# A gated recurrence on one core: the kept part of the state goes to TensorE as one fp32 operand, with idle passes and side work placed anew

## What is computed

```
x = x + ffn0(cond0(x))                       # token-wise, products over all tokens
def step(H, xs):                             # 128 steps, H is 16 x 128
    xz, xr, xh = xs                          # x times Wxz, Wxr, Wxh, with biases
    Z = sigmoid(xz + H @ Whz.T + bhz)
    R = sigmoid(xr + H @ Whr.T + bhr)
    H_tilda = tanh(xh + (R * H) @ Whh.T + bhh)
    H_new = Z * H + (1.0 - Z) * H_tilda
    Y = H_new @ Whq.T + bhq
    return H_new, Y
x = x + expert[argmax(Y @ router.T + b)](Y)  # relu(relu(Y w1 + b1) w2 + b2)
```

## Time and profile before

| | |
|---|---|
| median of three runs | 259.83 us (259.51 to 261.93) |
| the profiled execution | 263.02 us, its span 261.2 us |
| TensorE busy | 250.5 us of the span (96%), weight loads 204.6 (78%) |
| VectorE, ScalarE busy | 218.3 us (84%), 162.7 us (62%) |
| chain that ended last | TensorE 83%, VectorE 10%, ScalarE 3% of the span |
| granted TensorE clock | full from 9.7 to 20.0 us, half to 57.5 us, then full |
| first step's product with `parts`, step (1, 0)'s, step (7, 15)'s | 15.29, 54.68, 251.47 us |

### The profile page before, as it was taken

The page is one execution under the profiler, slowest core; times in us unless marked ns, Lnnn a source line. Parts: engine busy times, 40 slices in busy tenths (PEclk is TensorE's granted clock), DMA queues, the critical chain, the costliest instruction groups (busy, mean ns, idle before and its releaser), DMA issues.

```text
span 261.2 us, 10662 instructions
## 1 busy us (share of the span) xinstructions
PE 250.5 (96%) x3854; PEld 204.6 (78%) x3854; DVE 218.3 (84%) x1528; ACT 162.7 (62%) x826; POOL 15.2 (6%) x29
## 2 busy tenths in 40 slices
PE   6999899999999999999999999999999999999996
PEld 6978788788877788788877777777877777777775
DVE  5776566789998989988998999898988988788983
ACT  3455455557665866677666766587657766556652
POOL 4872000000000000000000000000000000000000
PEclk9995555559999999999999999999999999999999
DMA  7900000000000000000000000000000000000000
GB/s 245 360 15 6 0 3 1 3 0 4 4 3 4 23 1 3 4 24 3 4 4 20 4 3 4 4 23 4 3 1 23 4 4 3 21 5 0 5 23 23
DMA packets 3380, 5.76 MB, mean 22 GB/s; under 512 B 568, under 2 KB 2128, under 8 KB 3328
## 3 DMA queue, kind: packets, MB, share of 16 engines
q1 hardware_dynamic: 2848, 4.24, 4.8%
q10 hardware_dynamic: 432, 0.74, 0.8%
q0 software_dynamic: 48, 0.10, 0.1%
HBM read 4.03 MB, written 1.05 MB: 19 GB/s over the span
## 4 chain that ended last, share of the span: by engine, by line
PE 83%; DVE 10%; ACT 3%; issue 2%; DMA 2%; DVEq 0%
PE ZH L1087 9%; PE R L1087 8%; PE F L1010 6%; PE O L960 6%; PE ZH L1086 5%; PE O L957 3%; DVE parts L866 3%; PE O L916 3%; PE L L1097 2%; PE R L1132 2%; PE L L982 2%; PE O L953 2%; PE O L917 2%; PE O L918 2%; PE R L1086 2%
## 5 line engine op out<-in xcount | busy, mean ns | idle before, releaser
L454 ACT ACTIVATE r_early<-O 128x16 f32<-128x16 f32 x127 | 23.5, 185 | 35.0 <-PE O L960 32.0
L1087 PE MATMUL R<-m_p,gru_hi 128*128 128x16 f16 x254 | 44.2, 175 | 0.0
L487 ACT ACTIVATE ZH<-ZH 128x16 f32<-128x16 f32 x128 | 21.8, 170 | 29.9 <-PE ZH L1087 28.1
L1087 PE MATMUL ZH<-m_p,gru_hi 128*128 128x16 f16 x254 | 36.7, 170 | 0.0
L866 DVE TENSOR_TENSOR_SCAN parts<-factors,terms 128x48 f16<-128x48 f32 x128 | 33.0, 258 | 4.1 <-ACT factors L458 0.5
L837 DVE TENSOR_TENSOR terms<-r_early,factors 128x16 f16<-128x16 f32 x128 | 24.0, 188 | 12.7 <-ACT r_early L454 8.0
L609 DVE SCALAR_TENSOR_TENSOR hid_lo<-F,hid_hi 128x128 f16<-128x128 f32 x112 | 31.9, 285 | 0.2 <-issue 0.2
L458 ACT ACTIVATE factors<-R 128x16 f32<-128x16 f32 x128 | 24.7, 193 | 11.5 <-PE R L1087 0.2
L880 DVE TENSOR_TENSOR m_p<-keep,ZH 128x16 f16<-128x16 f32 x128 | 21.8, 170 | 11.4 <-ACT ZH L487 7.1
L482 ACT ACTIVATE keep<-z_sb 128x16 f32<-128x16 f32 x128 | 28.3, 221 | 2.1
L1086 PEld LDWEIGHTS ZH<-terms,gru_lo 128*128 128x128 f16 x128 | 12.7, 100 | 18.4 <-ACT z_sb L460 15.5
(11 more groups left out here) (270 smaller groups left out, 1057.3 us busy)
## 6 DMA issues: line engine op xcount, KB each, us to landing
w_sb<-w SPq DMA_DIRECT2D x2, 512.0 KB, 8.1
outT<-res SPq DMA_DIRECT2D x7, 128.0 KB, 1.9
xs_sb<-xsT SPq DMA_DIRECT2D x1, 640.0 KB, 9.7
first_sb<-first ACTq DMA_DIRECT2D x1, 279.0 KB, 4.0
ffn_sb<-ffn SPq DMA_DIRECT2D x1, 256.0 KB, 3.8
ffn_sb<-ffn ACTq DMA_DIRECT2D x1, 256.0 KB, 4.8
second_sb<-second SPq DMA_DIRECT2D x1, 256.0 KB, 4.5
xs_sb<-xsT SPq DMA_DIRECT2D x1, 256.0 KB, 6.7
```

What stands on the lines that cost most here:

```text
L454: nc.scalar.activation(r_early[:, p, :], early_r[:, at], ACT.Sigmoid).then_inc(early_made, 1)
L1087: return mm(out, gru_hi[:, WHR + gate, :], part, start=False, stop=low, skip_group_check=True)
```

## The change

- **zh whole.** VectorE makes zh in fp32 alone; its two fp16 parts and their tile fall away. TensorE multiplies it with the fp32 weights in one call each into the early copy, R and Z (`whole`): three fp32 matmuls of 16 columns in place of seven fp16 ones. The product into Z stands behind the first three of m, as the ones that it replaces did.
- **Chunk 0's idle passes.** `stream` passes are added ahead of the terms' product (`spare_first`), between the two candidate products and behind the last one; some numbers of `spare_passes` change.
- **Chunk 0's input.** From step 4 on the early copy's input is made from fp16 parts of x1, which ScalarE and VectorE make in two halves at steps 2 and 6 to 7 (`x1_first_high`, `x1_first_low`), with three matmuls in place of one fp32 one. Weight casts move by some steps for it.
- **Places of y and routing.** y's high part is taken behind the tanh, its low part's second half at step 2, the first places of the routing (`first_places`) both at step 5 ahead of the scan, the second `best_places` at step 4, x1 is evacuated in two halves at steps 6 and 7, and the low parts of the feed-forward layer move by half a step. Waits of TensorE on the O bank follow these (`out_bank_read`).

```diff
-                    nc.vector.tensor_tensor(zh_p[:, q, 0, :], z_sb[:, p, :], h_old, ALU.mult).then_inc(zh_hi, 1)
                     nc.vector.tensor_tensor(zh[:, q, :], z_sb[:, p, :], h_old, ALU.mult).then_inc(zh_full, 1)
                     wide_any(k, t, 0)
-                    dve.wait_ge(zh_full, step + 1)
-                    nc.vector.tensor_tensor(zh_p[:, q, 1, :], zh[:, q, :], zh_p[:, q, 0, :],
-                                            ALU.subtract).then_inc(zh_lo, 1)
...
+            def whole(out, gate, part):
+                mm(out, gru_sb[:, WHR + gate, :], part, start=False, stop=False, skip_group_check=True)
...
             def out_bank_read(k, t):
-                return t == {0: 4, K - 1: 0}.get(k, 6) or t == (12 if k == 0 else 0)
+                if k == 0 and t == 4:
+                    pe.wait_ge(x1_rest_made, 1)
+                if k > 1 and t == 0:
+                    pe.wait_ge(res_made, 2 * k - 3)
+                if k < K - 1 and t == (12 if k == 0 else 6):
+                    pe.wait_ge(x1_made, 2 * k + 2)
...
-                        if out_bank_read(k, t - 1):
-                            pe.wait_ge(zh_lo, step)
+                        out_bank_read(k, t - 1)
                         early_input(k, t)
-                        pe.wait_ge(zh_hi, step)
-                        early_product(t, zh_p[:, q, 0, :])
-                        product(r_out, 0, zh_p[:, q, 0, :])
-                        pe.wait_ge(zh_lo, step)
-                        product(r_out, 0, zh_p[:, q, 1, :], low=True)
+                        pe.wait_ge(zh_full, step)
+                        whole(early_r[:, at], 0, zh[:, q, :])
+                        whole(r_out, 0, zh[:, q, :])
                         pe.wait_ge(m_hi, step)
                         early_product(t, m_p[:, q, 0, :]).then_inc(early_mm, 1)
                         product(r_out, 0, m_p[:, q, 0, :])
                         pe.wait_ge(m_full, step)
-                        product(z_out, 1, zh_p[:, q, 0, :])
-                        product(z_out, 1, zh_p[:, q, 1, :], low=True)
+                        whole(z_out, 1, zh[:, q, :])
                         product(z_out, 1, m_p[:, q, 0, :])
...
-                if k == 0:
+                if k == 0 and t < 4:
                     mm(out, gru_sb[:, WXR, :], x1[:, at], start=False, stop=False, skip_group_check=True)
                 else:
+                    if k == 0 and t in (4, 8):
+                        pe.wait_ge(gru_lo_made, 2)
+                        pe.wait_ge(x1_first_lo, 1 + t // 8)
...
+            def spare_first(passes):
+                stream(L_bank[:, N:2 * N], passes)
             def first_before(t, step):
+                if t > 1:
+                    spare_first({2: 1, 3: 1, 6: 2, 7: 1, 12: 2, 13: 4}.get(t, 0))
...
             def first_between(t):
+                if t in (4, 10, 11, 12, 13):
+                    spare_first(1)
...
-                spare_passes(0, {7: 1, 8: 0, 9: 1, 12: 3, 13: 3}.get(t, 0))
+                spare_passes(0, (1, 1, 1, 1, 1, 1, 0, 1, 1, 1, 1, 1, 3, 3, 0, 0)[t])
...
+            def first_places(q):
+                dve.wait_ge(key_made, 2 * q + 2)
+                if q == 0:
+                    dve.wait_ge(zeros_set, 2)
+                for i in range(2):
+                    above(blocks(pen[:, i, :]), key[:, i:i + 1, :], best[:, i:i + 1]).then_inc(pen_made, 1)
...
+                        if t == 2:
+                            y_low(k - 1, 1)
                         if t == 4:
-                            first_place(k - 1, 0)
-                        if 7 <= t < 15:
+                            best_places(k - 1, 1)
+                        if t == 5:
+                            first_places(k - 1)
+                        if t == 7:
+                            x1_evacuate(k + 1, 1)
+                        if 8 <= t < 15:
                             expert_low(k - 1, t - 7, 0)
```

More of the change, by code:

```diff
@@ L380, in x1_high, with x1_first_high @@
             def x1_high(n):
-                act.wait_ge(x1_made, n + 1)
+                act.wait_ge(x1_made, 2 * n + 1)
                 nc.scalar.copy(x1_hi[:, n % 2, :], x1[:, cols(n)]).then_inc(x1_hi_made, 1)
+            def x1_first_high(half):
+                if half == 1:
+                    act.wait_ge(x1_rest_made, 1)
+                at = slice(half * 128, half * 128 + 128)
+                nc.scalar.copy(x1_hi[:, 0, at], x1[:, at]).then_inc(x1_first_hi, 1)
             def error_function(n):
@@ L471, in _ @@
                         w1_high(3)
-                    if feed and t == (13 if k == 0 else 7):
+                    if feed and t == (13 if k == 0 else 8):
                         x1_high(k + 1)
@@ L492, in _ @@
                         first_relu(1, 2 * t + 1)
-                    if k == 0 and t in (2, 3, 6):
-                        w1_high((2, 3, 6).index(t))
+                    if k == 0 and t == 2:
+                        x1_first_high(0)
+                    if k == 0 and t in (3, 6):
+                        w1_high((3, 6).index(t) * 2)
+                    if k == 0 and t == 15:
+                        w2_high(3)
                     if k == 0 and t == 4:
@@ L500, in _ @@
                         expander(t - 11)
+                    if experts and t == 0:
+                        y_high(k - 1)
                     if experts and t == (4 if last else 5):
@@ L535, in x1_first, with x1_first_low @@
                                                op1=ALU.add).then_inc(x1_rest_made if half else x1_made, 1)
+            def x1_first_low(half):
+                dve.wait_ge(x1_first_hi, half + 1)
+                at = of(half)
+                nc.vector.tensor_tensor(x1_lo[:, 0, at], x1[:, at], x1_hi[:, 0, at],
+                                        ALU.subtract).then_inc(x1_first_lo, 1)
             def low_rank_masked(n, half):
@@ L756, in first_wide @@
                     ffn_low(1, t - 8, half)
+                if t == 2 and half == 1:
+                    x1_first_low(0)
                 if t == 12 and half == 0:
                     dve.wait_ge(xs_next_in, 16)
-                    x1_evacuate(1)
+                    x1_evacuate(1, 0)
+                if t == 12 and half == 1:
+                    twice_gelu(2, 1)
                 if t == 14:
@@ L769, in wide @@
                     finish(k - 2, 0)
-                if t == 1:
-                    y_low(k - 1, half)
-                if 2 <= t < 2 + NF:
+                if t == 1 and half == 0:
+                    y_low(k - 1, 0)
+                if t == 1 and half == 1:
+                    ffn_low(k + 1, 0, 0)
+                if t == 2:
+                    ffn_low(k + 1, half, 1 - half)
+                if t == 3 and half == 0:
+                    best_places(k - 1, 0)
+                if t == 3 and half == 1:
+                    ffn_low(k + 1, 1, 1)
+                if t in (4, 5):
                     ffn_low(k + 1, t - 2, half)
-                if t == 3:
-                    best_places(k - 1, half)
-                if t == 4 and half == 0:
-                    first_place(k - 1, 1)
                 if t == 6 and half == 0:
@@ L780, in wide @@
                         dve.wait_ge(xs_in, 16)
-                    x1_evacuate(k + 1)
-                if 7 <= t < 15 and half == 0:
+                    x1_evacuate(k + 1, 0)
+                if k == 1 and t == 6 and half == 1:
+                    w2_low(7)
+                if t == 7:
+                    expert_low(k - 1, 0, half)
+                if 8 <= t < 15 and half == 0:
                     expert_low(k - 1, t - 7, 1)
-                if t in (7, 8) and half == 1:
-                    x1_low(k + 1, t - 7)
-                if t in (9, 10) and half == 1 and k < K - 3:
-                    low_rank_masked(k + 3, t - 9)
+                if t in (8, 9) and half == 1:
+                    x1_low(k + 1, t - 8)
+                if t in (10, 11) and half == 1 and k < K - 3:
+                    low_rank_masked(k + 3, t - 10)
                 if t in (12, 13) and half == 1 and k < K - 2:
@@ L801, in wide_last @@
                     best_places(K - 2, 1)
-                if t == 3 and half == 1:
-                    first_place(K - 2, 0)
                 if t - 1 in LAST_HIDDEN_AT and half == 0:
@@ L847, in _ @@
                         finish(k - 2, 1)
-                    if k == 0 and t in (12, 13):
-                        twice_gelu(2, t - 12)
                     if k == 0 and t in (14, 15):
@@ L853, in _ @@
                         first_early(t)
-                    if k == 1 and t in (0, 2, 6):
-                        w2_low((0, 2, 6).index(t) + 5)
+                    if k == 1 and t in (0, 1, 6):
+                        w2_low((0, 1, 6).index(t) + 4)
                     if last:
@@ L884, in _ @@
                                             ALU.subtract).then_inc(m_lo, 1)
+                    dve.wait_ge(zh_full, step + 1)
```

(2 more changed lines are left out.)

41 lines of the change are left out of this document (23 added, 18 removed).

## The result

The changed kernel takes 449.3 us (median of four runs, 445.53 to 450.19); the kernel before, on the same chip, takes 260.88 us (259.51 to 261.98). The ratio is 1.720 (95% interval 1.705 to 1.735). The forecast was 290 us with a range of 278 to 318, so slower was right and the size was not: the time lies 131 us beyond the range, at the end that the rival "The clock falls" had given as "up to 450 in all".

The account below looks back on a forecast made before the run. Bound by one chain through VectorE, TensorE and ScalarE, steps of 1.71 us. Profiled 263.0 us plus 33.2 for the 111 steps, minus 2.9 for chunk 0, is 293.3; less 3.2 without profile, 290 us, range 278 to 318.

Parts of the forecast that it names:

- The clock falls: Rival: TensorE drops to half clock; 309 us if in chunk 0, up to 450 if it stays low; chance 20%.
- What bounds the kernel: A single chain through VectorE, TensorE and ScalarE sets an ordinary step's 1.71 us; TensorE has only two small holes.
- the price of a call: Each fp32 matmul of 16 columns on TensorE costs 0.22 us at full clock, two passes of 0.11.
- Loads hidden: Rival: the fp32 passes' weight loads run under earlier matmuls on TensorE, giving 254 to 257 us; chance 6%.
- The step of 2.03: Three fp32 calls push R's last product 0.325 us later, so a step of 1.71 us becomes 2.03.
- The holes' account: TensorE's two holes in a step, 0.08 and some 0.09 us, take up 0.17 of the 0.49 us extra work.
- VectorE's two parts: Removing two VectorE instructions is worth nothing in ordinary steps, 0.1 to 0.2 us only in few steps.
- Moved side work: Both first places ahead of one scan cost 0.2 us in each of six chunks, 1.2 us; other moves nothing.
- Chunk 0: With the clock held at 2.4 GHz, its 16 steps take 36.5 us, a gain of 2.9.

Follow-up runs that it names:

- e1: The changed kernel with eight more idle passes on TensorE at step (0, 5), ahead of its wait; 412.92, 437.57, 414.59 and 345.89 us.
- e8: e5 with more idle passes in chunk 0, zh still in three fp32 calls; 292.73 us, ratio 1.116.
- e9: The changed kernel with seven fp16 products of zh in chunk 0, three fp32 calls from chunk 1 on, and e5's later passes; 286.18 us, ratio 1.091.
- e4: e1 with fp16 products of zh into the early copy and R, leaving only Z's fp32 call; 256.35 us, ratio 0.976.
- e2: The changed kernel with zh's seven fp16 products and VectorE's two parts put back, all else as changed; 250.95 us, ratio 0.954.
- e7: e2 plus four idle fp16 passes of 256 columns in each step where the fp32 calls stood; 280.62 us, ratio 1.069.
- e3: The kernel before with zh whole in three fp32 calls and waits on the O bank as changed, nothing else; 450.77 us, ratio 1.717.
- e6: e1 with two fp32 calls of zh, into the early copy and R, and fp16 products into Z; 396.42 us (345.11 to 397.56).
- e5: The changed kernel with more idle passes in chunk 0, at the later chunks' starts and ends, and in chunk 7; 412.77 us (344.43 to 460.33).

## Why the prediction was right or wrong

**What bounds the kernel; the price of a call.** Right. 0.45 and 0.23 us in the changed kernel at full clock, no hidden loads (the rival "Loads hidden" is out), and the chain behind R's last product unchanged (0.75 for 0.77).

**The step of 2.03.** Right in size: 2.01 in e1's chunk 1, in e8 and e9. The 111 steps take 228.35 us in e8, of which its passes at the chunks' ends are about 0.3 in each chunk (32.89 against 32.58 in e1's chunk 1); the forecast was 230.0. The holes' account was too simple, as e4 showed, but for three calls, two of them ahead of m, it comes out the same.

**VectorE's two parts.** Nothing gained, as said: with m's high part 0.32 us early in e8, VectorE isn't waited for.

**Moved side work.** I charged 1.2 us. e2 shows that together with all else but zh it brings 3.3 us in the 111 steps, of which 0.6 lie where before was still at half clock. Wrong in sign, small.

**Chunk 0.** This is the step that failed: "I take the clock as held: chunks 1 to 7 stay at 2.4 GHz throughout with side work of the same size in a step as chunk 0 now gets." The 111 steps were priced at full clock alone in the same way. Chunk 0 took 50.41 us for the 36.5 of the sum, the 111 steps 367.12 for its 230.0, at 1.2 GHz from 27.2 us on. Side work of the same size was beside the point. With as long a list in chunk 0, but passes in place of the fp32 calls, e7 does keep the clock there and takes 34.4 us, near the 36.5 forecast. The steps of chunks 1 to 7 that kept the clock had seven fp16 products of zh, and the change takes just these away. e3 shows the fp32 calls alone keep the clock from coming back; e7 shows that as long a list with fp16 passes holds it; e4 and e6 show that it turns between one call and two in a step. What the rows offered, and I passed over: before's one long stretch at half clock, 20.0 to 57.5 us, lies in the one chunk in which each step has an fp32 call of 16 columns, the early input. That is a hint and no more, since e4 has such a call in each step and keeps the clock. And I counted as evidence against the rival that the clock never fell in 193.8 us of later chunks, in none of which zh was fp32.

**The rival's number.** Its price was right; what would make the clock fall it didn't say. At half clock a call is 0.43 and the step 3.36 us, for the 3.4 given; a chunk costs 53.63 us against 32.58, 21 more, for the 22 given. That its "up to 450" comes so close to 449.3 is luck: 309 plus seven chunks at 22 is 463, while chunk 0 took 50.41 us for the 55 given and the seven chunks lost about 140 for the 154. What was wrong above all is its 20%, of which I gave half to a fall in chunk 0 alone or a late one, and so a range that ended at 318. Of the 170.3 us that the 111 steps lost, about 30 are the price at full clock (e8's 228.35 less some 2 for its own passes, against 196.79) and about 140 the clock's (367.12 against 226).

**The wait at step (0, 5).** The profile of after points at it, and the timeline of the fall begins there. e7 and e2's trace have the same wait at a held clock; e9 lost the clock right behind it, with fp16 products, and had it back 6.8 us later; e1 and e3 lost it ahead of the wait. It can be the moment of the fall. It is not what keeps the clock down for 409 us.

**Open.** Why e5 gets the clock back at the end of chunk 5 and e8 in chunk 0, with lists that differ by a few passes, and why one program (e1, e5, e6, e9) is at half clock for a different time from run to run, isn't settled. e5, e6 and e7 ran on another chip than the other experiments; the kernel before takes the same time on both (262.49 us there, 262.33 and 262.53 here). Which property of these fp32 calls costs the clock (the loads, the few columns, the two passes) wasn't tried apart.

## What to carry to other kernels

A step that runs at full clock tells nothing of the clock behind a change that replaces what TensorE does in it: price such a change at both levels, and give the lower one a chance of its own from the stretches of the trace in which the same kind of instruction already runs. Busy records are no evidence for the clock: 409.38 of 409.40 us here were at half. If a wait or a longer list seems to have lost the clock, put in passes of the same length in place of the suspected instructions; that one kernel (e7) separated time from kind.

## What the runs showed of the hardware

- Short fp32 matmuls can hold TensorE at 1.2 GHz for 409 us while its records show no idle time; fp16 passes of 256 columns that take as long keep 2.4 GHz (e7). The same fp32 calls also ran at 2.4 GHz for 262.7 us, behind idle passes (e8). The Trainium skill, in "TensorE: Matmul & The Clock Gate" under "Why this matters for your kernels", asks to keep TensorE busy and free of idle gaps to keep the clock; by the records this kernel does both, and the measurement goes against reading that rule from them.
- An fp32 matmul of 16 columns costs 0.22 us at 2.4 GHz and 0.43 us at 1.2 GHz, two passes of 0.11 and of 0.215. The Trainium skill, in the same page under "LDWEIGHTS (loading the stationary operand)", puts a weight load at its columns over 1.2, which makes an estimate of 107 ns for 128 columns; the pass at full clock agrees with this, and the pass at half clock is twice that, which the formula doesn't give. It is not what the fp16 products of 16 columns cost, which start some 0.025 us apart at either clock.
- The clock's state can differ from run to run of one program (e1: 345.89 to 437.57 us), and it can come back after a few idle passes, or not for 300 us.
